# Four graph layers on one core: ScalarE's own eviction word, wider table loads on TensorE, and eight constant float32 products per 16 steps

## The reference

```python
h = relu(layernorm(x)); x = x + L0(h, edges)      # softmax-weighted sum over a node's edges
h = relu(layernorm(x)); x = x + L1(h, src, dst)   # degree-normalized sum over edges, then a product
h = relu(layernorm(x)); x = x + L2(h, edge_attr)  # two small networks on every edge, summed both ways
h = relu(layernorm(x)); x = x + L3(h, edge_type)  # four steps of: sum of typed messages, then a GRU cell
```

## Time and profile before

| | us |
|---|---|
| median of three runs | 17633.98 |
| the profiled execution: its own time | 17631.68 |
| its span, first to last instruction | 17630.0 |
| build stage in it | 327.7 to 4226.0, 3898.3 long |
| PE busy, of the span | 11706.2 (66%) |
| DVE, ACT, POOL busy | 6523.6, 3405.9, 6218.5 |
| mean granted TensorE clock | 0.768 of full speed |

### The profile page before, as it was taken

How to read it: one execution, slowest core, us unless ns; L and a number is a source line. 1 busy time by engine, 2 the same in 40 slices (tenths; PEclk the granted TensorE clock), 3 DMA queues, 4 the chain that set the end, 5 groups by cost and what they waited for, 6 DMA issues and landing times.

```text
span 17630.0 us, 311796 instructions
## 1 busy us (share of the span) xinstructions
PE 11706.2 (66%) x67022; PEld 7502.6 (43%) x67023; DVE 6523.6 (37%) x30913; ACT 3405.9 (19%) x9727; POOL 6218.5 (35%) x6084
## 2 busy tenths in 40 slices
PE   2444444444554545567777677676777899999999
PEld 2222222222444444435555555555555444444443
DVE  6666666665333333333333333333332100000000
ACT  1333333332000000002222222222221000000000
POOL 2000000001455454507888888888883000000000
PEclk6555555555555555578999999999996999999999
DMA  2222222222111111153333333333335798989898
GB/s 93 80 84 81 83 83 81 85 83 80 34 35 35 34 35 34 35 217 37 42 41 42 41 41 41 42 41 41 42 41 45 300 344 331 342 330 341 332 342 309
DMA packets 1177918, 2115.01 MB, mean 120 GB/s; under 512 B 404316, under 2 KB 1020527, under 8 KB 1076671
## 3 DMA queue, kind: packets, MB, share of 16 engines
q1 hardware_dynamic: 828198, 1822.92, 29.7%
q0 software_dynamic: 348960, 284.02, 12.6%
HBM read 1647.55 MB, written 458.86 MB: 119 GB/s over the span
## 4 chain that ended last, share of the span: by engine, by line
PE 38%; issue 25%; POOL 13%; POOLq 9%; DVE 6%; another core or an unknown queue 4%; DMA 1%; DVEq 1%; ACT 1%; SPq 0%; ACTq 0%
PE ps L1365 13%; POOLq L749 9%; POOL G L466 7%; PE ps L1370 7%; POOL reverse L781 5%; PE ps L1081 5%; PE ps L1120 3%; PE ps L1110 2%; PE ps L1100 1%; DVE hots L1685 1%; DVE hots L1684 1%; PE ps L1307 1%; DVE hots L1683 1%; POOL scatter_hold L780 1%
## 5 line engine op out<-in xcount | busy, mean ns | idle before, releaser
L1081 PE MATMUL ps<-hots 128*128 128x392 f16 x4859 | 1781.7, 478 | 2116.1 <-ACT stagebuf L810 806.8
L781 POOL DMA_INDIRECT reverse<-SD,sidx x1660 | 2652.4, 1598 | 389.3 <-issue 378.4
L1365 PE MATMUL ps<-chunk,feat 128*128 128x512 f16 (+1 forms) x10192 | 2278.8, 375 | 14.4 <-DVE feat L2000 13.5
L464 POOL TENSOR_TENSOR hold_out<-hold_in 128x1 f32<-128x1 f32 x166 | 78.2, 471 | 5514.7 <-DMA idx<-index_table 4468.5
L1081 PEld LDWEIGHTS ps<-hots 128*128 128x128 f16 x4859 | 678.2, 140 | 2989.5 <-issue 2925.7
L810 ACT ACTIVATE stagebuf<-ps 128x392 f32 x3248 | 1377.4, 520 | 2551.9 <-POOLq L762 2549.8
L466 POOL DMA_INDIRECT G<-h_table,idx x1660 | 1653.4, 996 | 493.0 <-issue 488.8
L466 POOL DMA_INDIRECT G<-kv_table,idx x1660 | 1598.5, 963 | 518.2 <-issue 518.2
L1683 DVE TENSOR_SCALAR hots<-count_lo,key_lo 128x128 f16<-128x128 f16 x4859 | 1195.8, 246 | 1298.0 <-PE ps L1084 1297.2
L1854 DVE TENSOR_TENSOR acc<-acc,ps 128x132 f32 x1660 | 484.8, 292 | 3124.4 <-PE ps L1231 3066.5
L1228 PE MATMUL ps<-MS,OH 128*128 128x128 f32 x3320 | 782.0, 319 | 1260.9 <-issue 780.0
(11 more groups left out here) (392 smaller groups left out, 18054.9 us busy)
## 6 DMA issues: line engine op xcount, KB each, us to landing
chunk<-adj SPq DMA_DIRECT2D x720, 1792.0 KB, 9.0
adj<-stagebuf SPq DMA_DIRECT2D x406, 784.0 KB, 5.2
chunk<-adj SPq DMA_DIRECT2D x60, 1232.0 KB, 7.5
G<-in_edge SPq DMA_DIRECT2D x1660, 32.0 KB
G<-kv_table,idx POOLq DMA_INDIRECT x1660
G<-h_table,idx POOLq DMA_INDIRECT x1660
reverse<-SD,sidx POOLq DMA_INDIRECT x1660
reverse<-acc SPq DMA_DIRECT2D x4, 3225.0 KB, 20.0
```

The lines of the kernel that those rows point to most:

```text
L781: nc.gpsimd.indirect_dma_start(reverse[j % R], bass.IndirectOffsetOnAxis(sidx[:, j:j + 1], 0), SD[:, j % R, :], None, compute_op=ALU.add). ...
L1081: nc.tensor.matmul(ps[:, bass.ds(held["to"][j % STEPW], 2 * COMBS)], hots[:, j % BRING, 0:P], hots[:, j % BRING, P:P + 2 * COMBS], start=F ...
L1365: nc.tensor.matmul(bank[k % 2][:, 0:cols], feat[0][:, hi, 0:2, :].rearrange("p a d -> p (a d)"), columns(chunk4, i % DRING, m, cols), star ...
```

## The change

The change has three parts, all in the build stage and its tables.

1. *ACT waits by itself.* A semaphore `room_made` takes the place of `column_done`. POOL waits only for room in the staging buffer and loads one table row where it loaded two. ACT waits for `room_made` and then itself for `step_done`. Both of its numbers, the place in `stagebuf` and the step, come from one word: DVE shifts the place left by 13 bits (`ENDBITS`) and joins the step to it, two instructions over 3327 words of one partition at the prologue's end; a tenth DMA brings the row of steps to partition 96 (`endrow`).
2. *Wider loads on PE.* `STEPW` goes from 8 to 16: `to` and `clear` are loaded with 16 words once in 16 steps.
3. *Constant products on PE.* After the last step of each 16, PE does eight products of `ident` and 120 columns of `earlier`, both float32 and constant (`busy`, `WARM = 8`). They accumulate into the 120 words of a bank that no column uses, and nothing reads them. They stand ahead of the loop's branch and of the register loads of the next 16 steps.

```diff
-STEPW, VIRTW, BATCH = 8, 16, 4
+STEPW, VIRTW, BATCH = 16, 16, 4
+ENDBITS = 13
+WARM = 8
+        endrow = cmps[:, :, :].rearrange("p a b -> p (a b)")[96:97, 0:2 * VPAD].bitcast(I32)
# SP, after the three tables
-            sp.wait_ge(tab_loaded, 16 * 9)
+            sp.wait_ge(cmp_used, 3 * CG + VC)
+            sp.dma_start(endrow, virt_rows.rearrange("(q c) p -> q (c p)", q=3)[0:1, :]).then_inc(tab_loaded, 16)
+            sp.wait_ge(tab_loaded, 16 * 10)
# POOL, mark
-                    held["end"], held["ring"] = words(32, k + 1, BSTEPS), words(64, k, NEV + EPRE)
+                    held["ring"] = words(64, k, NEV + EPRE)
                 pool.wait_ge(events_done, held["ring"][j] & 255)
-                pool.wait_ge(step_done, held["end"][j] & 8191)
-                pool.sem_inc(column_done, 1)
+                pool.sem_inc(room_made, 1)
# ACT, evict
-                act.wait_ge(column_done, k + 1)
+                act.wait_ge(room_made, k + 1)
+                act.wait_ge(step_done, held["word"][j] & ((1 << ENDBITS) - 1))
                 nc.scalar.activation(
-                    stagebuf[:, bass.ds(held["to"][j], SLEN)]...
+                    stagebuf[:, bass.ds(held["word"][j] >> ENDBITS, SLEN)]...
# PE
+            aside = ps[:, 2 * COMBS:8 * 512]
+            def busy(n, j):
+                for _ in range(n):
+                    nc.tensor.matmul(aside[:, bass.ds(held["clear"][j], 512 - 2 * COMBS)], ident[:, :], earlier[:, 0:512 - 2 * COMBS],
+                                     start=False, stop=True, skip_group_check=True)
...
+                if j % STEPW == STEPW - 1:
+                    busy(WARM, j % STEPW)
# DVE, behind the masked keys
+            v.wait_ge(tab_loaded, 16 * 10)
+            place = virttab[96:97, 0:VPAD - 1]
+            nc.vector.tensor_scalar(place, place, ENDBITS, None, ALU.logical_shift_left).then_inc(word_made, 1)
+            v.wait_ge(word_made, 1)
+            nc.vector.tensor_tensor(place, place, endrow[:, 1:VPAD], ALU.bitwise_or).then_inc(word_made, 1)
+            v.wait_ge(word_made, 2)
```

More of the change, by code:

```diff
@@ L93 @@
 assert VPAD == 2 * SPAD
+assert BSTEPS < 1 << ENDBITS
 assert STEPS % HS == 0 and STEPS % SLOTS and HS % GR == 0 and U == UP == SLOTS and U % HALF == 0 and UGR % 2 == 0
@@ L358, in build @@
         key_masked, key_turned, key_copied = sem("key_masked"), sem("key_turned"), sem("key_copied")
-        hot_made, step_done, column_done, evicted, events_done = (
-            sem(n) for n in ("hot_made", "step_done", "column_done", "evicted", "events_done"))
+        hot_made, step_done, room_made, evicted, events_done = (
+            sem(n) for n in ("hot_made", "step_done", "room_made", "evicted", "events_done"))
         stored = [sem(f"stored{q}") for q in range(2)]
+        word_made = sem("word_made")
         built = sem("built")
@@ L744, in _ @@
                         .then_inc(key_gathered[h], 16)
-            pool.wait_ge(tab_loaded, 16 * 9)
+            pool.wait_ge(tab_loaded, 16 * 10)
             def words(row, k, top):
@@ L798, in _ @@
                 nc.scalar.activation(key_hi[:, lo:lo + n * P], bank[2 + q % 2][:, 0:n * P], ACT.Copy).then_inc(key_copied, 1)
-            act.wait_ge(tab_loaded, 16 * 9)
+            act.wait_ge(word_made, 2)
             held = {}
@@ L804, in evict @@
                 if j == 0:
-                    _, held["to"] = nc.values_load_multi_w_load_instructions(
+                    _, held["word"] = nc.values_load_multi_w_load_instructions(
                         virttab[96:97, k:k + VIRTW] if known(k) else virttab[96:97, bass.ds(k, VIRTW)], engines=(act.engine,),
-                        min_val=0, max_val=(SBUFS + OBUFS - 1) * SLEN + BLK - 2,
+                        min_val=1, max_val=((SBUFS + OBUFS - 1) * SLEN + BLK - 1 << ENDBITS) - 1,
                         skip_runtime_bounds_check_because="the path's tables are made of counts within these bounds")
-                act.wait_ge(column_done, k + 1)
+                act.wait_ge(room_made, k + 1)
+                act.wait_ge(step_done, held["word"][j] & ((1 << ENDBITS) - 1))
                 nc.scalar.activation(
-                    stagebuf[:, bass.ds(held["to"][j], SLEN)].rearrange("p (x c) -> p x c", c=BLK)[:, :, 0:2],
+                    stagebuf[:, bass.ds(held["word"][j] >> ENDBITS, SLEN)].rearrange("p (x c) -> p x c", c=BLK)[:, :, 0:2],
                     bank[j % 8][:, 0:2 * COMBS].rearrange("p (x c) -> p x c", c=2), ACT.Copy).then_inc(evicted, 1)
@@ L1057, in _ @@
                 last.then_inc(key_turned, 1)
-            pe.wait_ge(tab_loaded, 16 * 9)
+            pe.wait_ge(tab_loaded, 16 * 10)
             pe.wait_ge(key_copied, 10)
@@ L1669, in _ @@
                       op0=ALU.is_equal, op1=ALU.mult).then_inc(key_masked, 1)
+            v.wait_ge(tab_loaded, 16 * 10)
[4 more added lines that the diff above has]
+            v.wait_ge(word_made, 2)
             v.wait_ge(key_copied, 10)
-            v.wait_ge(tab_stored, 48)
             link(nc.vector.memset(zero16[:, :], 0.0))
```

## The result

The changed kernel takes 17444.94 us (median of four runs, 17441.28 to 17449.58); the kernel before takes 17633.6 us beside it. The ratio is 0.9895 with the interval 0.9877 to 0.9912: 188.7 us, 1.05%, faster. The forecast was 17515 us.

The account below looks back on a forecast made before the run. PE's own issue was taken to bound the build stage, with waits on ACT besides. A round summed to 12.45 us for 12.84, times 303.7 -118 us, +2 for the prologue: 17515 us, range 17270 to 17720.

Parts of the forecast that it names:

- ACT's own wait: Build stage: ACT no longer waits for POOL, so PE's waits on ACT go, -1.7 us a round of 16 steps.
- PE's waits on ACT under 100 us: Sign in the build stage: PE's waits for ACT, up to 806.8 us before, fall under 100 us.
- Wider loads: PE's register loads: two go, two double to 16 words at 1.1 us each; loads 3.37 us a round for 4.05.
- The stretching: PE's register loads taking longer while a block is stored: 1.0 us a round for 1.2, bounds 0.6 and 1.6.
- One gap for two: PE pauses once in 16 steps, DVE's eight sets run out: +1.3 us a round, steps 5.86 us for 4.5.
- The eight products: Constant products behind each 16 steps on PE: 0.92 us a round, held by the queue.
- Branch and register operations: PE's sequencer between two groups of 16 steps: 1.3 us a round.
- The clock: Build stage: granted clock rises above 0.56; DVE's release at most 0.15 us earlier, 45 us in all, counted as nothing.
- The prologue: Two DVE instructions over 3327 words, partly under the wait for ACT's copies: +2 us in all.
- the quiet round: Sign: a round of 16 steps on PE without stretched loads takes 11.3 to 11.6 us, longer than 10.0 before.
- the slower one: Rival at PE's sequencer between groups: gap and products outweigh the wait removed, round 13.8 us, +290 us, 17920 us; chance 0.20.
- Cheap loads: Rival: a 16-word load on PE takes 0.76 us, round 11.2 us, minus 490 us, 17140 us; chance 0.26.

Follow-up runs that it names:

- word_only: The kernel before with only ACT's own wait (8-word loads, no constant products): ratio 0.9694 to the kernel before, -508 us.
- word_wide: The changed kernel without the eight constant products, so ACT's own wait and 16-word loads: ratio 0.9883 to the kernel before, -192 us.
- ring16: The changed kernel with sixteen sets in DVE's ring instead of eight: ratio 0.9732 to the kernel before, -447 us.
- word_warm8: The changed kernel with 8-word loads, so ACT's own wait and the eight products once in 16 steps: ratio 0.9764 to the kernel before, -390 us.
- products_only: The kernel before with the eight constant products alone: ratio 1.0010 to the kernel before, +16 us.
- wide_only: The kernel before with the 16-word loads alone, ACT still waiting for POOL: ratio 1.0083 to the kernel before, +141 us.
- packed_free: word_only, with every fourth word of row `free` copied once so PE's four-word load reads adjoining words: ratio 0.9538 to the kernel before, -767 us.
- double_store: word_only, with each block stored a second time to a spare table: ratio 0.9934 to the kernel before, -112 us.
- after_again: The changed kernel run once more as reference on the experiments' chips: ratio 0.9890 to the kernel before, -186 us.

## Why the prediction was right, point by point

The round forecast at 12.45 us came out at 12.22, 0.23 us or 70 us less. By its steps:

- **ACT's own wait, -1.7 us a round** (bounds -1.2 and -2.7). Right, and closely: word_only's stage is 1.68 us a round shorter, and the sequencer of the kernel before waits 1.75 us a round for banks. The remainder after quiet issue and stretched loads was the true size. The 806.8 us of the earlier trace rows were not.
- **PE's waits on ACT under 100 us.** By the row it is 140.5, but the sequencer's wait for banks is 7 us, and the rest of that row lies in waits for DVE's sets. The step itself held.
- **Wider loads, 1.1 us each.** Mis-sized: 1.109 and 1.280 us. With the first load the three take 3.56 us for 3.37, +0.19 a round. The bounds held. The stretching was taken as 1.0, less than the 1.2 before, and measures 1.29, +0.29: it did not shrink with the number of loads.
- **One gap for two, +1.3 us** (bounds 0.8 and 1.6). Right. The steps of word_wide take 6.01 us for word_only's 4.65: 1.37 us for the refill. ring16 takes it out again, and 0.25 more. The sixteen steps were put at 5.86 us and take 5.97, with the waits in the third and fourth batch, as foretold.
- **The eight products, 0.92 us.** Mis-sized, and the largest miss: one register operation serves all eight, as their offset is the same. From the last step to the branch it is 0.43 us for 0.21 without products, so they cost 0.21 us a round, -0.71. I had reasoned from count steps, each of which has an offset of its own. That the queue holds them free of charge was right only where the engine is not behind: the same products hold the sequencer 0.36 us in word_warm8 and products_only and some 0.59 in ring16, which no term of mine covers.
- **Branch and register operations, 1.3 us.** 0.21 behind the last step and 1.00 ahead of the first are 1.22 (rounded): -0.1.
- **The clock, nothing.** Right: it goes from 0.56 to 0.78 (0.79 in word_warm8), and no kernel with products is faster than the one without. The release of DVE at the high clock came 0.49 us after PE for 0.66, about the 0.15 us allowed, but only after 112 of the 304 pauses; after the others it is 0.66 as before. The first product of the next group shows the clock fallen there: it takes 0.51 us after the long gap (at 2011.63) and 0.34 after the quiet one (at 2022.63).
- **The prologue, +2 us.** The two instructions take 1.89 and 3.62 us, and most of it lies under ACT's copies. In the total this can't be told from scatter.

```profile
296.04 1.89 DVE L1690 TENSOR_SCALAR path<-path 1x3327 int32<-1x3327 int32 x1
297.96 3.62 DVE L1692 TENSOR_TENSOR path<-path,cmps 1x3327 int32<-1x3327 int32 x1
```

The terms add up: 5.97 + 0.21 + 1.22 + 3.56 + 1.29 = 12.25 us, where the mean round from branch to branch is 12.24.

The mechanism was thus right in its parts: a gain of 510 us, of which the single gap, the change's own second part, takes 312 back. That the total is off by only 70 us is partly luck, since two errors of size have opposite signs. Removing ACT's wait gave what was forecast. The wide loads were to cost 1.3 - 0.68 - 0.2 = 0.42 us a round and cost 1.03 (312 us), 0.61 more. The products were to cost 0.92 and cost 0.03 (8 us) in the time, 0.89 less. Two signs that the prediction names did not appear for this reason: the quiet round is 10.8 to 10.9 us and not 11.3 to 11.6, and the gap between groups is 4.9 us when quiet; it comes near the 6.5 only in the mean (6.27, with stretched loads). What hid this balance from the result is its sum. Of the rivals, the slower one had its place right (PE's sequencer between two groups) and is what wide_only shows, +138 us, where no wait of ACT is removed. It fell on the products' price. Cheap loads fell on 1.109 and 1.280 us.

## What to carry to other kernels

When an engine's busy time is low and its waits are few, read its sequencer's rows from branch to branch: here the round was register loads, branches and the issue of steps, so a faster clock was worth next to nothing. Products in the shadow of the loads cost what time they hold the sequencer: 0.21 to 0.59 us a round, the more the further the engine lags behind it. Two stalls that a buffer covers one by one can't be joined into one unless the buffer grows with them; the same edit cost 312 us with eight sets and gained 104 with sixteen (and the packed row). Run each part alone before accepting a sum: the change as a whole takes 185 us out of the stage where one of its parts takes 510. And where a view puts a wait down to an engine, look at the gap between the sequencer's two operations: 140.5 us "for ACT" were 7.

## What the runs showed of the hardware that I had not expected

- **Spacing of words in a register load.** Four words, each four apart, take 1168 ns on PE; four adjoining ones 339 ns in packed_free. The Trainium skill ("DMA: Bandwidth & Descriptors", section "Latency and other measured facts") gives such a load a floor of about 600 ns. The row lies under it, and the spaced load far above it: the place of the words counts for more than their number.
- **A load slows with store traffic.** In the kernel after the first load of a round takes up to 3717 ns in the gap shown, where it takes 1169 when quiet, and double_store doubles the excess. All of PE's loads over 1.4 us in the kernel before ran while DMAs moved data. ACT's loads took 1.0 us throughout, but none of them ran beside a store, so they say nothing on this.
- **POOL's load.** The first load of POOL's block took 7.18 us in the kernel before. In the kernel after, the one that is left takes 2.15 us (and ACT's the usual 1.02):

```profile
L756 POOLq TENSOR_LOAD <-path x2: 2152/2156/2161, 2007.2 to 2028.8; - x2
...
L811 ACTq TENSOR_LOAD <-path x2: 1019/1022/1024, 2002.6 to 2024.1; - x2
```

  What made it 7.18 us was not tried. The transfers show that in the kernel before this load ran beside a store each time (224 GB/s in the median), and the 1.24 us load behind it never. But the 2.15 us load of the kernel after runs in the same traffic, so a store alone does not make 7.18 us.
- **One stage of the same program differs by 1037 us between sets of runs.** The products of the attention stage, in the kernel after and in after_again:

```profile
L1137 PE MATMUL ps<-MS,OH x3320: 269/421/481, 4153.6 to 7372.6; 128*128 128x66 f32 x196
```

```profile
L1137 PE MATMUL ps<-MS,OH x3320: 420/421/482, 4142.0 to 6324.4; 128*128 128x66 f32 x196
```

  3219 and 2182 us, with equal products and the clock at 0.50 in both. The gathers of POOL take 0.96 and 1.01 us each. Only their rhythm differs. In the long one POOL stands before 80 of its 83 groups of 20 gathers, and in the short one never:

```profile
POOL hold_out L469 <- DVE MS L1776: 1054.3, 80, 13.6
```

  These 1054.3 us are about the difference. What holds the consumers of the gathers back there stays open, and so does whether it is the chip that makes it: two sets of runs, on two chips, have the short stage, and two the long one.
